# A message-passing layer on one core: pairs of edge blocks share a loaded stretch of the node table, and PE's general path is moved behind the body's code

## The chip, the cores and the metric

One core of a Trainium2 chip runs the whole kernel. Its engines are TensorE (PE in the profile), VectorE (DVE), ScalarE (ACT), GpSimd (POOL) and SyncE (SP), which here only starts transfers. The metric is device time in microseconds of one execution, without the profiler: the median of several runs. The profile is one further execution with the profiler on.

## The reference

6250 nodes with 128 features, 100,000 edges sorted by `dst` (`dst = int(6250 * u**2)` for uniform u, so low nodes have many edges and the last ones about 8 each), `src` at random. In short:

```python
row, col = edge_index                     # src, dst
h = relu(concat(x[row], x[col]) @ Wm1 + bm1)      # hidden 256
h = relu(h @ Wm2 + bm2)
messages = h @ Wm3 + bm3
agg = segment_sum(messages, col) / clip(count, 1.0)[:, None]
upd = relu(concat(x, agg) @ Wn1 + bn1) @ Wn2 + bn2
out = layernorm(x + (x + upd))
```

## The kernel before

**Tables first.** `Wm1` is split by rows, so that the first layer of a message is A[src] + B[dst], with A and B products of x. The prologue makes `a_table` (256 values a node) and `b_table` (two parts, high and low, of 256 values a node, so two table rows a node) in DRAM, in groups `g` of 4 x 128 nodes, one loop of all engines over `g`. In between it reads the edges, turns `dst` into numbers relative to each block's lowest node and into words that later steer the loops.

**Edges in.** Edges are cut into blocks of `EB` = 256, 391 of them (`NBE`), padded to 392 (`NB`). They are loaded into `edges_in` with block `g * BG + p` in partition `p`, column group `g` (`GR` = 4 groups, `BG` = 98 blocks in each). The list `loads` (L444 to 455) cuts `dst` and `src` into transfers of up to 98 rows, and SP issues them at L479, after the first three loads of x. POOL waits for all of them at L607, converts both to floats (L608 source, L612 destination), and DVE takes the lowest and highest node of each block from that (`first_and_last`, L824 and L827, in its step g = 2, ahead of its other work for that group). DVE also makes `rel16`, destination less the block's lowest (`make_relative`, L849), and the words `words_sp`, `words_act`, `words_pe`, `words_dve` (`ranges_and_spans`, L891 to 898, and what follows). SP stores minimum and maximum to `mm_dram` (L518), fetches them back as one row (L522), and stores `rel16` to `rel_dram` (L526).

**The body** takes the blocks in turn, `U` = 4 in one pass of a hardware loop; passes 0, 1 and the last are written out apart (`bodies`). For block k:

- SP loads the pair's relative destinations `rel` (on even k, L543) and the 128 table rows (64 nodes) from the block's lowest node on into `b_win[k % 4]` (L547), when PE has expanded block k - 4 (`s_ex`; an even block waits for k - 3 too, since `rel` is shared by the pair).
- POOL gathers `a_table` rows by `src`, 128 edges in one indirect transfer, two for a block (L630), when block k - 4 has been expanded.
- DVE compares `rel` with the node numbers of the window and gets `onehot_t` (`make_onehot_t`, L1023), two blocks ahead.
- PE transposes the gathered rows into a PSUM bank (L1413) and adds `b_win` x `onehot_t` (`expand`, L1324): the first layer.
- ACT applies relu (`h1`, L732), DVE takes the low part (L1106); PE multiplies by `Wm2` in parts (L1437, 12 matmuls, for block k - 2); ACT and DVE again relu (L740) and low part (L1118); ACT puts the bias in the next bank ahead (L721).
- PE sums edges by node: `onehot` (DVE, L1038) times h2, for block k - 6, four matmuls (L1341, L1345, L1347, L1349) into one of two banks of `sums`, until the block's range of nodes ends. Then PE goes on in the other bank, and DVE adds the old one to `agg` (L1060).

**Far windows.** A block whose nodes span more than the 64 of its window has `far` = (highest - lowest) >> 6 above 0. For each further 64 nodes ACT loads another 128 table rows into `b_far` (`load_far`, in the step before), DVE makes another one-hot at the end of its step, PE waits for both (`expand_far`) and adds two more matmuls.

**PE's word.** One word per block tells PE all exceptions together: far windows of block k, a range that ended before block k - 6, ranges after that. If it is 0 only the straight path is needed:

```python
with pe.If(word > 0):        # L1418
    expand_and_sum(i, k, word)          # the general path
with pe.If(word < 1):        # L1420
    expand(...); first_sum(...); other_sums(...)
```

After the blocks, the end computes the node update and the layernorm in groups g.

Of the kernel before, what the change touches and what calls it, by code (L numbers as in the profile page):

```python
# [34 lines left out]
def gnn_layer(nc, x, src, dst, Wm1, bm1, Wm2, bm2, Wm3, bm3, Wn1, bn1, Wn2, bn2, out):  # L35
# [25 lines left out]
    with ExitStack() as ctx:  # L61
# [20 lines left out]
        words_sp = sb("words_sp", [1, NB], I32)  # L82
# [91 lines left out]
        row_more = carve(NB).bitcast(I32)  # L174
        row_step, row_end = carve(NB).bitcast(I32), carve(NB).bitcast(I32)
# [8 lines left out]
        minmax_i = carve(2 * GR).bitcast(I32)  # L184
        first_quarter = carve(GR).bitcast(I32)
# [47 lines left out]
        s_mm = sem("s_min_max")  # L233
        s_wi = sem("s_min_max_int")
# [27 lines left out]
        s_bw = [sem(f"s_b_win_loaded{c}") for c in range(RB)]  # L262
# [198 lines left out]
        def _(sp):  # L461
# [15 lines left out]
            for n, g, row, rows, edges in loads:  # L477
                at, e0 = (n * GR + g) * EB, (g * BG + row) * EB
# [26 lines left out]
            for g in range(1, NG + 1):  # L505
# [9 lines left out]
                if g == 3:  # L515
                    sp.wait_ge(s_wi, 1)
                    for j in range(GR):
                        sp.dma_start(mm_dram[j * BG:(j + 1) * BG, :], minmax_i[0:BG, 2 * j:2 * j + 2]  # L518
                                     ).then_inc(s_scr, 16)
                if g == 4:  # L520
                    sp.wait_ge(s_scr, 16 * GR)
                    sp.dma_start(row_in[0:1, :], mm_dram.rearrange("(o b) c -> o (b c)", o=1)).then_inc(s_row, 16)  # L522
                if g == 5:
                    sp.wait_ge(s_rel16, 1)
                    for j in range(GR):
                        sp.dma_start(rel_dram[j * BG:(j + 1) * BG, :],  # L526
                                     rel16[0:BG, j * EB:(j + 1) * EB]).then_inc(s_scr_rel, 16)

            sp.wait_ge(s_scr_rel, 16 * GR)
# [7 lines left out]
            def body(i):  # L537
                first = load_words(sp, words_sp, i * U, U, PAD_DST)
                for k in range(U):
                    if there(i, k - RB):  # L540
                        sp.wait_ge(s_ex, i * U + (k - RB + (2 if k % 2 == 0 else 1)))
                    if k % 2 == 0:
# [971 lines left out]
```

## Time and profile before

| | |
|---|---|
| median of 3 runs | 1201.61 us (1199.98 to 1201.78) |
| the profiled execution, its span from first to last instruction | 1416.6 us |
| granted TensorE clock, mean | 0.993 |
| PE busy | 1249.7 us, 88% |
| weight loads of PE busy | 1172.0 us, 83% |
| DVE busy | 979.6 us, 69% |
| ACT busy | 740.6 us, 52% |
| POOL busy | 786.5 us, 56% |
| moved by the DMA engines | 211.4 MB, mean 149 GB/s |

The profiled execution is 215.0 us longer than the median of the runs; it has no other time than its span. Busy is the time in which the engine has at least one instruction of its own at work. The share of the chain is the part of the span that the last chain of dependent work spent on an engine; "issue" in it is time in which the engine waited for nothing that the profile shows. In the timeline, a row is one instruction or a run of like ones, with start, duration, and in brackets the idle time before it.

### The profile page before, as it was taken

Reading aid. Unit: us, or ns where it says so; the run is one execution under the profiler, and the core shown is the slowest. Engines: PE = TensorE matmul, PEld = TensorE weight load, DVE = VectorE, ACT = ScalarE, POOL = GpSimd, SP = SyncE. Lnnn points to the kernel's source line nnn. Section 1 sums busy time; section 2 is a strip of 40 time slices with the busy share of each in tenths; the row PEclk is TensorE's granted clock in tenths of the full one; section 3 lists DMA queues with packets and bytes.
Section 4 is the critical chain, followed back from the end, with each engine's and each line's share of the span. In section 5 each row is a group of like instructions: output and inputs, shape, how many; then the busy total and the mean of one; then the engine's idle time right before and its main releaser. Section 6 shows DMA issues by size and latency. Waiting matters only on the chain.

```text
span 1416.6 us, 33766 instructions
## 1 busy us (share of the span) xinstructions
PE 1249.7 (88%) x9614; PEld 1172.0 (83%) x9615; DVE 979.6 (69%) x2072; ACT 740.6 (52%) x1392; POOL 786.5 (56%) x814
## 2 busy tenths in 40 slices
PE   6978888888888888888888889988999989899997
PEld 6868888888888888888888888888888888888886
DVE  6846666766766666766766766767767767777676
ACT  3544555555555555555555555555554555545585
POOL 2166666666666666666666666666666666564000
PEclk9999999999999999999999999999999999999999
DMA  9665555545545555555545555455545454554022
GB/s 308 274 234 156 146 144 151 149 141 151 151 140 150 152 142 147 151 143 147 152 139 150 146 143 151 145 144 152 139 147 151 138 150 144 145 151 142 10 67 86
DMA packets 135605, 211.42 MB, mean 149 GB/s; under 512 B 24247, under 2 KB 102669, under 8 KB 134030
## 3 DMA queue, kind: packets, MB, share of 16 engines
q1 hardware_dynamic: 98030, 108.43, 25.3%
q0 software_dynamic: 37536, 102.55, 25.1%
q8 instruction: 14, 0.23, 0.1%
q14 instruction: 25, 0.20, 0.0%
HBM read 188.09 MB, written 22.80 MB: 149 GB/s over the span
## 4 chain that ended last, share of the span: by engine, by line
PE 80%; issue 12%; DVE 2%; SPq 1%; another core or an unknown queue 1%; DMA 1%; ACT 1%; DVEq 1%; ACTq 0%
PE bank L1437 39%; PE bank L1413 11%; PE bank L1324 6%; PE sums L1345 4%; PE sums L1341 4%; PE sums L1347 3%; PE sums L1349 3%; PE bank L1478 2%; PE sums L1491 1%; PE bank L1234 1%; PE bank L1219 1%; PE bank L1461 1%; PE sums L1219 1%; DMA b_win<-b_table 1%
## 5 line engine op out<-in xcount | busy, mean ns | idle before, releaser
L630 POOL DMA_INDIRECT a_edge<-a_table,src_idx x782 | 767.1, 981 | 457.8 <-remote 268.2
L1437 PE MATMUL bank<-w,h 128*128 128x256 f32 x4692 | 661.4, 283 | 104.9 <-issue 102.1
L1437 PEld LDWEIGHTS bank<-w,h 128*128 128x128 f32 x4692 | 596.5, 188 | 119.7 <-issue 118.7
L1106 DVE SCALAR_TENSOR_TENSOR h<-bank,h 128x512 fp32r<-128x512 f32 x391 | 268.7, 687 | 338.4 <-issue 326.7
L732 ACT ACTIVATE h<-bank 128x512 fp32r<-128x512 f32 x391 | 233.8, 598 | 475.3 <-remote 439.2
L721 ACT COPY bank<-b_bc 128x512 f32<-128x512 f32 x391 | 231.5, 592 | 115.2 <-issue 66.7
L1118 DVE SCALAR_TENSOR_TENSOR h_lo<-bank,h_hi 128x512 fp32r<-128x512 f32 x391 | 266.5, 681 | 0.1
L1413 PE MATMUL bank<-ident,a_edge 128*128 128x128 f32 x1564 | 237.4, 274 | 21.1 <-issue 16.6
L740 ACT ACTIVATE h_hi<-bank 128x512 fp32r<-128x512 f32 x391 | 232.6, 595 | 2.8 <-PE bank L1437 2.8
L1413 PEld LDWEIGHTS bank<-ident,a_edge 128*128 128x128 f32 x1564 | 180.3, 140 | 40.5 <-issue 34.2
L1324 PE MATMUL bank<-onehot_t,b_win 128*128 128x256 f32 x782 | 190.3, 325 | 0.0
L1038 DVE SCALAR_TENSOR_TENSOR onehot<-iota,first_node,dst_col 128x256 fp32r<-128x256 int16 x391 | 186.0, 476 | 0.4 <-PE sums L1349 0.3
L1023 DVE TENSOR_SCALAR onehot_t<-rel,node_half 128x256 fp32r<-128x256 int16 x391 | 154.7, 396 | 22.0 <-DMA rel<-rel_dram 2.9
L1341 PE MATMUL sums<-h_hi,onehot 128*128 128x258 f32 x391 | 115.8, 296 | 15.0 <-issue 12.3
L1324 PEld LDWEIGHTS bank<-onehot_t,b_win 128*128 128x128 f32 x782 | 118.6, 192 | 3.3 <-issue 1.0
L1345 PE MATMUL sums<-h_lo,onehot 128*128 128x256 f32 x391 | 116.3, 298 | 1.0
L1347 PE MATMUL sums<-h_hi,onehot 128*128 128x258 f32 x391 | 110.4, 282 | 0.0
L1349 PE MATMUL sums<-h_lo,onehot 128*128 128x256 f32 x391 | 109.6, 280 | 0.0
L1341 PEld LDWEIGHTS sums<-h_hi,onehot 128*128 128x128 f32 x391 | 73.4, 188 | 25.1 <-issue 24.8
L1345 PEld LDWEIGHTS sums<-h_lo,onehot 128*128 128x128 f32 x391 | 73.7, 189 | 13.0 <-issue 12.6
L1347 PEld LDWEIGHTS sums<-h_hi,onehot 128*128 128x128 f32 x391 | 74.2, 190 | 0.0
L1349 PEld LDWEIGHTS sums<-h_lo,onehot 128*128 128x128 f32 x391 | 73.4, 188 | 0.0
(190 smaller groups left out, 682.7 us busy)
## 6 DMA issues: line engine op xcount, KB each, us to landing
b_win<-b_table SPq DMA_DIRECT2D x391, 128.0 KB
rel<-rel_dram SPq DMA_DIRECT2D x196, 128.0 KB
a_edge<-a_table,src_idx POOLq DMA_INDIRECT x782
a_table<-work SPq DMA_DIRECT2D x12, 512.0 KB, 4.6
b_table<-work SPq DMA_DIRECT2D x5, 1024.0 KB
b_table<-h SPq DMA_DIRECT2D x4, 1024.0 KB
f_x<-in_x SPq DMA_DIRECT2D x12, 256.0 KB, 5.2
b_table<-a_edge SPq DMA_DIRECT2D x3, 1024.0 KB, 5.8
```

What stands on the lines that cost most here:

```text
L630: pool.indirect_dma_start(a_edge[:, b % R * TB + t, :], None, a_table, bass.IndirectOffsetOnAxis(ap=src_idx[:, b * TB + t:b * TB + t + 1], ...
L721: act.copy(bank[H2[k % U]][:, :], b2_bc[:, :, :].rearrange("p t h -> p (t h)")).then_inc(s_bias, 1)
L732: act.activation(h1[:, k % U, 0, :], bank[k % 2][:, :], ACT.Relu).then_inc(s_h1h, 1)
L740: act.activation(h2_hi[:, (k - LAG) % U, :, 0:H], bank[H2[(k - LAG) % U]][:, :].rearrange("p (t h) -> p t h", t=TB), ACT.Relu).then_inc(s_ ...
L1106: dve.scalar_tensor_tensor(h1[:, k % U, 1, :], bank[k % 2][:, :], 0.0, h1[:, k % U, 0, :].bitcast(F32), ALU.max, ALU.subtract).then_inc(s_ ...
L1118: dve.scalar_tensor_tensor(h2_lo[:, j, :, :], bank[H2[j]][:, :].rearrange("p (t h) -> p t h", t=TB), 0.0, h2_hi[:, j, :, 0:H].bitcast(F32) ...
L1324: ins = pe.matmul(bank[k % 2][:, h * EB:(h + 1) * EB], rows[:, h * P:(h + 1) * P], hot, start=False, stop=True, skip_group_check=True)
L1341: return pe.matmul(to[:, 0:HC], onehot[:, slot, 0, :], h2_hi[:, k % U, 0, :], start=start, stop=False, skip_group_check=True)
L1345: pe.matmul(to[:, 0:H], onehot[:, slot, 0, :], h2_lo[:, k % U, 0, :], start=False, stop=False, skip_group_check=True)
L1347: pe.matmul(to[:, 0:HC], onehot[:, slot, 1, :], h2_hi[:, k % U, 1, :], start=False, stop=False, skip_group_check=True)
L1413: ins = pe.matmul(bank[k % 2][:, h * EB + t * P:h * EB + (t + 1) * P], a_edge[:, k % R * TB + t, h * P:(h + 1) * P], ident[:, :], start=(t ...
L1437: ins = pe.matmul(to, h1[:, j, a, h * EB + t * P:h * EB + (t + 1) * P], w2[:, b, h, :], start=False, stop=(a == 1 and h == KH - 1), skip_g ...
```

## The change

Four things are done. The 128-row stretch of `b_table` is loaded once for two blocks, from the lower of their lowest nodes, and `rel16`, `words_sp` and `far` are taken relative to that. The edges lie in `edges_in` with two neighbouring blocks side by side in one partition, and so are loaded in rows of 512 edges; the stores to `mm_dram` and `rel_dram` become two each. ACT's copies of the transposed edges are rearranged to match. And on PE the general path is emitted after the straight code of the whole pass, reached by a branch, with a branch back.

```diff
-        full = E // EB
-        assert (GR - 1) * BG <= full
+        full = E // (2 * EB)
+        assert (GR // 2 - 1) * BG <= full < GR // 2 * BG
         loads = []
         for n in range(2):
-            for g in range(GR):
-                rows = min(full - g * BG, BG)
+            for a in range(GR // 2):
+                rows = min(full - a * BG, BG)
                 if rows:
-                    loads.append((n, g, 0, rows, EB))
-            if E % EB:
-                loads.append((n, GR - 1, rows, 1, E % EB))
+                    loads.append((n, a, 0, rows, 2 * EB))
+            if E % (2 * EB):
+                loads.append((n, GR // 2 - 1, rows, 1, E % (2 * EB)))
...
-            for n, g, row, rows, edges in loads:
-                at, e0 = (n * GR + g) * EB, (g * BG + row) * EB
+            for n, a, row, rows, edges in loads:
+                at, e0 = (n * GR + 2 * a) * EB, (a * BG + row) * 2 * EB
...
-                    for j in range(GR):
-                        sp.dma_start(mm_dram[j * BG:(j + 1) * BG, :], minmax_i[0:BG, 2 * j:2 * j + 2]
-                                     ).then_inc(s_scr, 16)
+                    for a in range(GR // 2):
+                        sp.dma_start(mm_dram[a * 2 * BG:(a + 1) * 2 * BG, :].rearrange("(p c) m -> p (c m)", c=2),
+                                     minmax_i[0:BG, 4 * a:4 * a + 4]).then_inc(s_scr, 16)
...
-                first = load_words(sp, words_sp, i * U, U, PAD_DST)
-                for k in range(U):
-                    if there(i, k - RB):
-                        sp.wait_ge(s_ex, i * U + (k - RB + (2 if k % 2 == 0 else 1)))
...
+                first = load_words(sp, words_sp, i * (U // 2), U // 2, PAD_DST)
+                for c in range(RC):
+                    if there(i, 2 * c - U):
+                        sp.wait_ge(s_ex, i * U + (2 * c - U + 2))
+                    sp.dma_start(rel[:, c, :].rearrange("p (b e) -> p b e", b=2),
+                                 rel_dram[bass.ds(i * U + 2 * c, 2), :].partition_broadcast(P)
+                                 ).then_inc(s_rc[c], 16)
+                    sp.dma_start(b_win[:, c, :].bitcast(F32),
+                                 b_table[bass.ds(first[c] * 2, P), :]).then_inc(s_bw[c], 16)
...
-            pool.memset(edges_in[:, (GR - 1) * EB:GR * EB], PAD_DST).then_inc(s_pad, 1)
-            pool.memset(edges_in[:, (2 * GR - 1) * EB:2 * GR * EB], 0).then_inc(s_pad, 1)
+            pool.memset(edges_in[:, (GR - 2) * EB:GR * EB], PAD_DST).then_inc(s_pad, 1)
+            pool.memset(edges_in[:, (2 * GR - 2) * EB:2 * GR * EB], 0).then_inc(s_pad, 1)
...
+                dve.tensor_tensor(pair_low[0:BG, :], minmax[0:BG, 0:2 * GR:4], minmax[0:BG, 2:2 * GR:4], ALU.min
+                                  ).then_inc(s_mm, 1)
...
-                dve.tensor_copy(words_sp[0:1, :], lowest).then_inc(s_rw, 1)
-                dve.tensor_tensor(far, highest, lowest, ALU.subtract).then_inc(s_rw, 1)
+                dve.tensor_tensor(words_sp[0:1, :], row_in[0:1, 0:2 * NB:4], row_in[0:1, 2:2 * NB:4], ALU.min
+                                  ).then_inc(s_rw, 1)
+                dve.tensor_tensor(row_low[0:1, :].rearrange("o (b c) -> o b c", c=2),
...
+                dve.wait_ge(s_low, 1)
+                dve.tensor_tensor(far, highest, row_low[0:1, :], ALU.subtract).then_inc(s_rw, 1)
...
                 if k % 2 == 0:
                     dve.wait_ge(s_rc[k // 2 % RC], nth(i, k, 16))
-                dve.wait_ge(s_bw[k % RB], nth(i, k, 16))
+                    dve.wait_ge(s_bw[k // 2 % RC], nth(i, k, 16))
...
-                        with pe.If(word > 0):
-                            expand_and_sum(i, k, word)
-                        with pe.If(word < 1):
-                            expand(b_win[:, k % RB, :], onehot_t[:, k % 2, :], k).then_inc(s_ex, 1)
...
+                        outer[k] = nc.cur_bb
+                        pe.br_cmp(word, 0, on_true=label(i, k, "apart"), on_false=label(i, k, "straight"),
+                                  comp_op="IS_GT")
+                        nc.switch_bb(label(i, k, "straight"), parent=outer[k])
+                        expand(b_win[:, k // 2 % RC, :], onehot_t[:, k % 2, :], k).then_inc(s_ex, 1)
+                        to = bank_at(own)
+                        first_sum(to, (k - BACK) % U, k - BACK, False)
+                        ins = other_sums(to, (k - BACK) % U, k - BACK)
+                        if among_last(i, k - BACK, BACK + 1):
+                            ins.then_inc(s_sg, 1)
+                        pe.br(label(i, k, "joined"))
+                        nc.switch_bb(label(i, k, "joined"), parent=outer[k])
...
+                last = nc.cur_bb
+                pe.br(label(i, 0, "ended"))
+                for k in steps(i, BACK + 1):
+                    if there(i, k) and there(i, k - BACK - 1):
+                        with nc.body(label(i, k, "apart"), parent=outer[k], valid_engines=bass.OrderedEngineSet([pe.engine])):
+                            expand_and_sum(i, k, words[k])
+                            pe.br(label(i, k, "joined"))
+                nc.switch_bb(label(i, 0, "ended"), parent=last)
```

The stores to `rel_dram` change as those to `mm_dram` do.

## Rows read from the trace of the kernel before

**Rows 1.** The page, parts 1 and 4: busy time, and the chain that ended last.

```profile
PE 1249.7 (88%) x9614; PEld 1172.0 (83%) x9615; DVE 979.6 (69%) x2072; ACT 740.6 (52%) x1392; POOL 786.5 (56%) x814
...
PE 80%; issue 12%; DVE 2%; SPq 1%; another core or an unknown queue 1%; DMA 1%; ACT 1%; DVEq 1%; ACTq 0%
```

**Rows 2.** Windows: stretch, its length, busy time (count), granted clock, DMA share, GB/s.

```profile
core 0: us, PE busy (x) PEld busy (x) DVE busy (x) ACT busy (x) POOL busy (x), PEclk, DMA share, GB/s
0.00:89.40 89.40, 69.46 (x446) 62.58 (x447) 63.73 (x115) 41.92 (x79) 24.89 (x37) 0.96 0.81 293
89.40:1308.00 1218.60, 1081.74 (x8533) 1023.51 (x8534) 840.62 (x1673) 632.09 (x1164) 760.61 (x776) 1.00 0.51 147
...
600.75:602.35 1.60, 0.37 (x1) 0.19 (x1) 0.52 (x1) 0.00 (x0) 0.74 (x1) 1.00 0.72 230
```

**Rows 3.** Timeline of PE in the body: start, duration, line, operation.

```profile
628.18 0.48 PE L1324 MATMUL bank<-onehot_t,b_win 128*128 128x256 f32 x2
...
628.98 1.58 PE L1437 MATMUL bank<-w,h 128*128 128x256 f32 x12
...
631.54 0.28 PE L1437 MATMUL bank<-w,h 128*128 128x256 f32 x1
```

**Rows 4.** The groups view (part 5 of the page): count, busy, mean ns, idle before.

```profile
L630 POOL DMA_INDIRECT a_edge<-a_table,src_idx x782 | 767.1, 981 | 457.8 <-remote 268.2
...
L1324 PE MATMUL bank<-onehot_t,b_win 128*128 128x256 f32 x782 | 190.3, 325 | 0.0
...
L1023 DVE TENSOR_SCALAR onehot_t<-rel,node_half 128x256 fp32r<-128x256 int16 x391 | 154.7, 396 | 22.0 <-DMA rel<-rel_dram 2.9 <-DMA b_win<-b_table 1.6 <-issue 0.7
```

**Rows 5.** Timeline of the engines over two blocks of the body.

```profile
605.33 0.95 POOL L630 DMA_INDIRECT a_edge<-a_table,src_idx  x1 [0.30 <-issue]
605.43 0.59 ACT L721 COPY bank<-b_bc 128x512 f32<-128x512 f32 x1 [0.75 <-issue]
...
605.55 0.48 PE L1324 MATMUL bank<-onehot_t,b_win 128*128 128x256 f32 x2
...
606.72 0.68 DVE L1118 SCALAR_TENSOR_TENSOR h_lo<-bank,h_hi 128x512 fp32r<-128x512 f32 x1
```

**Rows 6.** The DMA view: count, KB each, median us from issue to landing.

```profile
f_x<-in_x SPq DMA_DIRECT2D x12, 256.0 KB, 5.2
...
a_table<-work SPq DMA_DIRECT2D x1, 128.0 KB, 3.5
...
f_x<-in_x SPq DMA_DIRECT2D x1, 53.0 KB
```

**Rows 7.** The lines of PE's two branches: durations ns, least, median, most.

```profile
L1418 PEldq COMPARE_BRANCH  x384: 68/204/338, 108.2 to 1307.6; - x192
...
L1420 PEldq COMPARE_BRANCH  x384: 72/73/202, 108.6 to 1307.9; - x192
```

**Rows 8.** The DMA view from 130 to 1300 us: queues, packets, MB, share.

```profile
q1 hardware_dynamic: 80681, 73.48, 22.1%
q14 instruction: 5, 0.04, 0.0%
```

**Rows 9.** Windows of the prologue, columns as in rows 2.

```profile
10.00:15.00 5.00, 5.00 (x40) 5.00 (x40) 3.13 (x5) 2.25 (x4) 2.03 (x2) 1.00 1.07 342
...
15.00:30.00 15.00, 9.73 (x69) 9.07 (x67) 12.58 (x22) 6.42 (x15) 0.00 (x0) 0.89 1.03 391
```

**Rows 10.** Timeline of the prologue, POOL and DVE.

```profile
11.48 1.04 POOL L608 CAST agg<-a_edge 98x1024 f32<-98x1024 int32 x1 [5.07 <-DMA a_edge<-in_src]
...
13.54 0.70 DVE L824 TENSOR_SCALAR agg<-a_edge 98x1024 int32<-98x1024 int32 x1 [0.33 <-POOL agg L612]
...
23.28 1.29 DVE L979 TENSOR_TENSOR work<-bank,rel 128x512 f32<-128x512 f32 x2 [2.18 <-DMA a_table<-work]
```

**Rows 11.** Timeline of the prologue, DVE's work on one row.

```profile
39.65 0.55 DVE L893 TENSOR_TENSOR agg<-agg 1x392 int32<-1x392 int32 x1
```

**Rows 12.** Timeline of SP's queue in the prologue: issues.

```profile
26.26 5.35 SPq L518 DMA_DIRECT2D mm_dram<-agg  x4
...
38.82 3.12 SPq L526 DMA_DIRECT2D rel_dram<-agg  x4
```

More of the change, by code:

```diff
@@ L184, in gnn_layer @@
         minmax_i = carve(2 * GR).bitcast(I32)
+        pair_low = carve(GR // 2)
         first_quarter = carve(GR).bitcast(I32)
@@ L233, in gnn_layer @@
         s_mm = sem("s_min_max")
+        s_low = sem("s_lowest_of_pairs")
         s_wi = sem("s_min_max_int")
@@ L261, in gnn_layer @@
         s_rc = [sem(f"s_rel_loaded{c}") for c in range(RC)]
-        s_bw = [sem(f"s_b_win_loaded{c}") for c in range(RB)]
+        s_bw = [sem(f"s_b_win_loaded{c}") for c in range(RC)]
         s_bf = sem("s_b_far_loaded")
@@ L524, in _ @@
                     sp.wait_ge(s_rel16, 1)
[L525 to L529, printed above, removed]
+                    for a in range(GR // 2):
+                        sp.dma_start(rel_dram[a * 2 * BG:(a + 1) * 2 * BG, :].rearrange("(p c) e -> p (c e)", c=2),
+                                     rel16[0:BG, a * 2 * EB:(a + 1) * 2 * EB]).then_inc(s_scr_rel, 16)
+            sp.wait_ge(s_scr_rel, 16 * (GR // 2))
             sp.wait_ge(s_bz, 16)
@@ L537, in body @@
             def body(i):
-                first = load_words(sp, words_sp, i * U, U, PAD_DST)
-                for k in range(U):
-                    if there(i, k - RB):
-                        sp.wait_ge(s_ex, i * U + (k - RB + (2 if k % 2 == 0 else 1)))
-                    if k % 2 == 0:
-                        sp.dma_start(rel[:, k // 2, :].rearrange("p (b e) -> p b e", b=2),
-                                     rel_dram[bass.ds(i * U + k, 2), :].partition_broadcast(P)
-                                     ).then_inc(s_rc[k // 2], 16)
-                    if there(i, k):
-                        sp.dma_start(b_win[:, k % RB, :].bitcast(F32),
-                                     b_table[bass.ds(first[k] * 2, P), :]).then_inc(s_bw[k % RB], 16)
+                first = load_words(sp, words_sp, i * (U // 2), U // 2, PAD_DST)
[7 more added lines that the diff above has]
+                                 b_table[bass.ds(first[c] * 2, P), :]).then_inc(s_bw[c], 16)
             bodies(sp, body)
@@ L645, in edge_columns @@
                     act.wait_ge(s_et, n * GR + g // 2 * 2 + 2)
-                    act.copy(col[:, g * BG * TB:(g + 1) * BG * TB].rearrange("p (b t) -> p t b", t=TB),
+                    act.copy(col[:, g // 2 * 2 * BG * TB:(g // 2 + 1) * 2 * BG * TB]
+                             .rearrange("p (b c t) -> p c t b", c=2, t=TB)[:, g % 2, :, :],
                              bank[6 + g // 2][:, g % 2 * TB * BG:(g % 2 + 1) * TB * BG]
@@ L847, in make_relative @@
             def make_relative():
-                dve.tensor_tensor(rel16[0:BG, :].rearrange("p (g e) -> p g e", g=GR), dst_f,
-                                  minmax[0:BG, 0:2 * GR:2].unsqueeze(2).to_broadcast([BG, GR, EB]), ALU.subtract
+                dve.wait_ge(s_mm, 3)
+                dve.tensor_tensor(rel16[0:BG, :].rearrange("p (a e) -> p a e", a=GR // 2),
+                                  dst_f.rearrange("p (a c) e -> p a (c e)", c=2),
+                                  pair_low[0:BG, :].unsqueeze(2).to_broadcast([BG, GR // 2, 2 * EB]), ALU.subtract
                                   ).then_inc(s_rel16, 1)
@@ L902, in first_words @@
                 dve.wait_ge(s_rw, 6)
-                dve.scalar_tensor_tensor(words_act[0:1, 0:NB], far, float(2**13), lowest, ALU.mult, ALU.add
+                dve.scalar_tensor_tensor(words_act[0:1, 0:NB], far, float(2**13), row_low[0:1, :], ALU.mult, ALU.add
                                          ).then_inc(s_rw, 1)
@@ L1402, in expand_and_sum, with label @@
                     sum_all_further(k - BACK - 1, word)
+            def label(i, k, what):
+                return f"pe_body{i if isinstance(i, int) else 'loop'}_block{k}_{what}"
             def body(i):
                 words = load_words(pe, words_pe, i * U, words_of(i, BACK + 1), PE_TOP)
+                outer = {}
                 for k in steps(i, BACK + 1):
```

16 lines of the change are left out of this document (8 added, 8 removed).

## The prediction

> **What bounds the kernel now.** I read the page first: TensorE (PE) is busy 88% of the span and holds 80% of the chain that ended last, with 12% put down to "issue" [rows 1]. So I asked what PE does in a block and what the "issue" is. The windows give three stages: a prologue of 89.4 us that builds the tables, a body of 391 blocks until 1308.0, and an end of 108.6 us [rows 2]. PE's timeline in the body shows a block without a hole: L1437 begins at 628.98 and again at 631.54, 2.56 us, matmuls back to back between [rows 3]; I call such blocks free, and take 2.57. But the body's mean is 1218.6/391 = 3.12 us. The difference, some 214 us, sits in pauses in which all engines stop at once: between 600.75 and 602.35 PE begins one matmul, VectorE (DVE) ends one operation and ScalarE (ACT) does nothing [rows 2]. PE then resumes within a batch of L1437, which waits for no semaphore, so no dependency of the kernel explains it. The runs' median, 1201.61 us, is 215.0 us below the profiled span of 1416.6, and 89.4 + 391 x 2.57 + 108.6 = 1202.9: the runs outside the profiler are what the trace gives without its pauses. So PE bounds the body at 2.57 us a block, and the body has next to nothing to win unless a matmul goes. None does. The terms below are microseconds of a stage; I add them to the profiled span and to the median alike, without scaling.
>
> GpSimd (POOL) is close behind PE: two gathers a block of 981 ns, and 0.30 between [rows 4, 5], 2.56 us. DVE has 840.6/391 = 2.15 us a block [rows 2].
>
> **The change part by part.**
>
> *Half the loads of the node table.* 195 loads of 128 KB go. DVE waited 1.6 us in all for a loaded window [rows 4], the DMA engines are 51% busy in the body [rows 2]: the loads lie under PE's matmuls. Were the body bound by the gathers instead, fewer loads would not shorten POOL's 981 ns. Bounds 0 and -2 us; I take 0.
>
> *A pair's second block reaches beyond 64 nodes.* The window starts at the lower of two lowest nodes. From the reference's inputs I worked out `(highest - lowest of the pair) >> 6`: it is 1 for blocks 383, 387 and 389, and 0 for the rest; before it was 0 for all, as L1324's 782 = 2 x 391 matmuls say [rows 4]. Each of the three now takes the far path: ACT loads 128 KB, DVE makes one more one-hot after its step, PE waits for both and runs two more matmuls. In a free stretch PE wants the next expansion at 605.55, while DVE is done with its step at 606.72 + 0.68 = 607.40 and needs 0.40 for the one-hot [rows 4, 5]: 2.25 us late. ACT's COPY begins at 605.43 [rows 5]; behind it ACT reads its word and issues, and a 128 KB transfer landed in 3.5 us at the quickest [rows 6]: some 4 us late. PE is the bound, so its wait stays. Bounds for one: 0.24 us (all covered, two matmuls of 0.12) and 4.5 us; I take 3, so 3 x 3 = +9 us, bounds +1 and +14.
>
> *PE's general path behind the body's code.* In the records of PE's sequencer L1418 takes 204 ns, jumping over the general path, and L1420 73 ns [rows 7]. The new straight block keeps one untaken compare and at most one plain branch: 0.2 us less, 316 times. In free blocks that lies under matmuls issued before it: from L1324 on there is no hole [rows 3]. The blocks that end a range (62 before, 65 now, worked out from the inputs) take a jump of 204 ns there and one back, +0.2 us each, under the same matmuls. Sum 0. Bounds: all straight jumps exposed -63 us, for which the 1202.9 against 1201.6 leaves no room; all general ones exposed +13 us.
>
> A rule speaks against this edit. Between 130 and 1300 us the queue that brought PE's code in 16 KB pieces carries nothing, and the other code queue 0.04 MB [rows 8], though PE jumps back over the whole body every fourth block. By these rows a jump to the end of the body costs 0.2 us and no transfer. The Trainium skill (Runtime: NRT & Kernel Launch, Instruction fetch mechanics) says that a taken branch to code outside a window of two pages waits for a DMA. That is rival 4, priced there from rows.
>
> *Edge loads in pairs of blocks.* Here is what I expect to decide. Before, `dst` and `src` each come in loads of 98, 98, 98, 96 and 1 rows of 256 edges. After, 100000/512 = 195 rows of 512 edges are cut into 98, 97 and 1. What matters is over how many DMA engines a load is spread. The trace's semaphore events say it: a 128-row load of x raises its semaphore 16 times as data lands; the load of x's last 106 rows raises it once at issue and twice on landing, at 20.00 and 20.17; the ten edge loads raise theirs 126 times, which is 6 x (14 + 1) + 2 x 16 + 2 x (1 + 1). So 128 rows use 16 engines, 98 use 14, 96 use 16, 106 use 2 and 1 uses 1: the largest divisor up to 16. (The DMA view gives a landing for the 256 KB loads and none for the 53 KB one [rows 6], since it looks for 16 steps.) 97 is prime: one engine carries 97 x 2 KB = 199 KB, twice.
>
> An engine's rate: all 16 at full share move 342 to 391 GB/s [rows 9], 21.4 to 24.4 each. 199 KB take 8.1 to 9.3 us, two in a row 16.3 to 18.6. Before, 800 KB over all engines took 50 KB each, 2.0 to 2.3 us. So the edges are complete 14 to 16.5 us later than now, less up to 1.5 for four SP issues that go. If the two run on different engines it is 6 to 7 us. No row decides which; nothing in the trace shows engines taking turns, so I take the same engine, +14 us.
>
> Who waits: POOL's L608 waits for all edge loads; it waited 5.07 us already and began at 11.48. DVE's L824 stands behind it at 13.54 with 0.33 us to spare [rows 10], and DVE goes in order: the rest of group 2 (the low part of x, the copies of both products) is queued behind it, and PE behind that. Later transfers queue on the same engine, above all the store of a_table whose landing ended DVE's wait of 2.18 us at 23.28 [rows 10]; it moves along. DVE is busy 12.58 of 15 us from 15 on [rows 9], so little can be caught up. I keep all 14.
>
> The Trainium skill (DMA: Bandwidth & Descriptors, Why a DMA increments its semaphore by 16 and not by 1) states the same divisor rule and that HWDGE takes the lowest-numbered engines. The trace's counts agree with the first; the second no row shows. By the page the sum would be the same.
>
> *The rest of the prologue.* DVE gets a minimum of 98x4, one over 196 in place of a copy over 392, and one over 392 like L893, 0.55 us [rows 11], with its wait: +1 us in all, DVE being on the path (bounds 0 and +1.5). Two stores fewer to `mm_dram` and two to `rel_dram`, where SP spent 5.35 and 3.12 us on four each [rows 12], under PE's and DVE's work: -1 to 0, I take -0.6. POOL's two larger memsets end before SP comes to wait for them: 0.
>
> Sum: 1201.6 + 14 + 9 + 1 + 0 - 0.6 = 1225.0. A little may be caught up; I say **1224 us**.
>
> **The rivals.**
> 1. *The two prime loads run side by side*: +6 in place of +14, so 1217. For it: no row names the engine. Chance 0.12.
> 2. *The edges are no problem*: the 97 rows are cut otherwise. Then +9 and +1: 1211, or 1203 with the far blocks at their low bound. Against it: the 106-row load. 0.08.
> 3. *Faster*: PE's sequencer, not the matmuls, bounds the body outside the profiler. What decides is the share of the 316 straight jumps that is exposed: all give -63 us, and from 26 us on (0.4 of them) it outweighs the rest; with 40 us, 1184. Against it: [rows 3] and the sum of 1202.9. 0.11.
> 4. *General blocks pay for the far jump*: 65 x 0.2 = +13, 1237; with a code transfer each of 3.5 us, like the quickest of [rows 6], +228, 1452. Against it: [rows 8]. 0.06.
>
> The forecast has 0.63.
>
> **How the numbers follow.** A measurement of this kernel tells about 0.2%, 2.4 us. The likeliest case by its bounds: 1201.6 + 12 + 1 - 1 = 1214 to 1201.6 + 16.5 + 14 + 1.5 = 1234. To hold eight in ten I go down over rival 1 and most of 2 to 1206 and up to 1237. Faster 0.12 (rival 3 and a little of 2), same 0.05 (the low end of 2 and a partial 3), slower 0.83.
>
> **What would show it.** After the change L608 starts near 25 us, its wait ended by a load of `src`, and the body's first transposes near 104, not 89.4. Free blocks stay at 2.57 us. L1324's successor has 788 matmuls, with holes of 2 to 4 us before the far ones. There are 196 window loads. The prediction is wrong if L608's successor starts before 16 us, if free blocks fall under 2.5, or if the body grows by more than 14 us.

## The result, and the profile after

The kernel after takes **1241.47 us** (median of 4 runs, 1240.39 to 1243.82) against 1201.69 (1199.98 to 1201.94) on the same chip: a ratio of 1.0332, 95% interval 1.0318 to 1.0347. It is slower, as predicted, but by 39.8 us instead of 22, outside the range (1206 to 1237).

The page of the kernel after, its busy times and its chain (they answer to [rows 1]):

```profile
PE 1183.9 (95%) x9620; PEld 1158.4 (93%) x9621; DVE 962.5 (78%) x2077; ACT 742.0 (60%) x1392; POOL 771.6 (62%) x814
...
PE 90%; DMA 4%; DVE 2%; issue 2%; POOL 1%; SPq 1%; ACT 0%; DVEq 0%; ACTq 0%
```

This profile has no pauses: its span of 1240.3 us is the run's own time less 1.9. So the difference can't be read against the profile of before with its 215 us of pauses. I took a new profile of the kernel before (first experiment); its span is 1200.1. Windows of the kernel after, cut at the first transposes of blocks 0, 20, 380 and 390 (columns as in [rows 2]):

```profile
0.00:104.47 104.47, 71.81 (x446) 64.32 (x448) 64.36 (x117) 43.13 (x79) 24.86 (x36) 0.87 0.68 250
...
104.47:157.44 52.97, 49.86 (x393) 48.82 (x393) 36.79 (x74) 30.88 (x56) 39.28 (x42) 0.94 0.54 153
157.44:1088.34 930.90, 930.69 (x7923) 927.56 (x7922) 763.63 (x1556) 586.04 (x1080) 692.37 (x721) 1.00 0.53 152
1088.34:1133.19 44.85, 33.65 (x228) 31.94 (x227) 25.35 (x53) 16.36 (x31) 14.11 (x15) 0.85 0.38 103
...
1133.19:1240.30 107.11, 97.89 (x638) 85.75 (x636) 72.32 (x279) 65.58 (x147) 0.99 (x2) 0.98 0.17 54
```

and of the new profile of the kernel before, cut at the same blocks:

```profile
0.00:88.72 88.72, 69.09 (x447) 62.23 (x448) 63.71 (x115) 41.97 (x79) 24.59 (x37) 0.96 0.81 295
...
88.72:140.49 51.77, 49.30 (x393) 48.35 (x394) 36.40 (x74) 30.78 (x56) 39.39 (x41) 0.93 0.62 183
140.49:1066.65 926.16, 926.16 (x7922) 926.15 (x7921) 767.67 (x1556) 594.85 (x1080) 700.67 (x721) 1.00 0.61 178
1066.65:1092.47 25.82, 25.82 (x222) 25.78 (x221) 22.21 (x46) 16.46 (x30) 14.44 (x15) 1.00 0.62 181
...
1092.47:1200.10 107.63, 98.47 (x638) 85.90 (x636) 74.22 (x283) 66.26 (x149) 0.99 (x2) 0.98 0.17 54
```

Read the first number after each stretch, its length. The prologue is 15.8 us longer, blocks 0 to 19 are 1.2, blocks 20 to 379 are 4.7, **the ten blocks from 380 are 19.0 us longer**, the end is 0.5 shorter: 40.2 us. The last ten also show PE at a granted clock of 0.85. The prologue is what was predicted; the body was to grow by 9 us and grows by 25.

*The prologue.* POOL's first cast of the edges, two rows of SP's queue (the three issues for `src`, and the next load of x), and DVE's step that waits for a store of a_table (they answer to [rows 10]):

```profile
25.49 1.04 POOL L609 CAST agg<-a_edge 98x1024 f32<-98x1024 int32 x1 [18.66 <-DMA a_edge<-in_src]
...
5.24 10.31 SPq L482 DMA_DIRECT2D a_edge<-in_src  x3
15.59 0.36 SPq L467 DMA_DIRECT2D f_x<-in_x  x1
...
37.05 1.29 DVE L991 TENSOR_TENSOR work<-bank,rel 128x512 f32<-128x512 f32 x2 [1.87 <-DMA a_table<-work]
```

The cast begins 14 us later than in [rows 10]. In the trace's semaphore events, the edges' semaphore takes 38 steps, 2 x (14 + 1) + 4 x (1 + 1): each 97-row load uses one engine. Its steps pause between 16.35 and 25.23 us, 8.9 us, before the last two: the second of these loads lands that much behind the first.

*The first block of the last pass.* PE's timeline, and behind it the view of the branch's line in PE's sequencer, for this block (durations in ns, least, median, most; first and last start):

```profile
1115.46 0.60 PE L1430 MATMUL bank<-ident,a_edge 128*128 128x128 f32 x4
1121.19 0.80 PE L1336 MATMUL bank<-onehot_t,b_win 128*128 128x256 f32 x2 [5.13 <-issue]
...
1123.29 2.76 PE L1458 MATMUL bank<-w,h 128*128 128x256 f32 x12
```

```profile
L1436 PEldq COMPARE_BRANCH  x1: 5444/5444/5444, 1115.3 to 1115.3; - x1
```

That is block 388, and it ends a range: PE stands 5.13 us at "issue", because its sequencer's jump to the general path took 5.4 us. L1458's twelve matmuls then take 2.76 us instead of 1.58: the granted clock was at the lower level after the hole (0.50 from 1121.2 to 1126 us). It is not a far block. The queue that brings PE's code in 16 KB packets, silent from 136 to 1117 us, shows in the DMA view from 1100 to 1135:

```profile
q8 instruction: 5, 0.08, 1.1%
```

The first of the five packets begins at 1118.4 us, within the jump. Block 389's branch takes 5.2 us too, from 1123.0 on, with packets that begin at 1124.2 and 1124.7.

*A block of the loop that ends a range and begins a pass* (block 56), in the kernel after and in the new profile of before, PE's first three sums:

```profile
250.72 0.34 PE L1353 MATMUL sums<-h_hi,onehot 128*128 128x258 f32 x1
251.07 0.38 PE L1357 MATMUL sums<-h_lo,onehot 128*128 128x256 f32 x1
251.29 0.28 PE L1359 MATMUL sums<-h_hi,onehot 128*128 128x258 f32 x1
```

```profile
233.77 0.29 PE L1341 MATMUL sums<-h_hi,onehot 128*128 128x258 f32 x1
233.89 0.28 PE L1345 MATMUL sums<-h_lo,onehot 128*128 128x256 f32 x1
234.01 0.28 PE L1347 MATMUL sums<-h_hi,onehot 128*128 128x258 f32 x1
```

From the start of the first to the start of the third it is 0.57 us after and 0.24 before, and the block takes 2.90 us. There are 16 such blocks in the loop, all of them 2.84 to 2.92 us, and they are the 4.7 us of the middle. Blocks that end a range elsewhere in a pass cost nothing more.

*The far blocks.* PE, DVE and ACT at block 383, and PE's groups (they answer to [rows 4]):

```profile
1098.81 0.66 PE L1336 MATMUL bank<-onehot_t,b_far 128*128 128x256 f32 x2 [2.16 <-DVE onehot_t L1042]
...
1097.39 0.49 DVE L1072 SCALAR_TENSOR_TENSOR agg<-sums,from_quarter,agg  x1
1098.33 0.35 DVE L1042 TENSOR_SCALAR onehot_t<-rel,node_half 128x256 fp32r<-128x256 int16 x1 [0.45 <-issue]
...
1095.63 0.40 ACTq L719 DMA_DIRECT2D b_far<-b_table  x1
```

```profile
L1336 PE MATMUL bank<-onehot_t,b_win 128*128 128x256 f32 x782 | 189.8, 324 | 5.1 <-issue 5.1
L1336 PE MATMUL bank<-onehot_t,b_far 128*128 128x256 f32 x6 | 1.7, 363 | 5.9 <-DVE onehot_t L1042 3.7 <-issue 2.2
```

788 matmuls and three holes, as predicted. Blocks 383, 387 and 389 are 4.2, 2.3 and 4.8 us longer than 2.57, but 389's hole is put down to "issue": its branch of 5.2 us ended last, most of it under the slow matmuls of block 388. With the path back in the body (inline, below) DVE's one-hot ends 389's hole, which is as long (2.12 us), and the block is still 4.3 us longer: most of it is the far window's.

### The profile page after: what moved, and what is told of

The parts are those of the page before. It is cut to its first block, busy times and chain, and to the rows that moved or that the text cites. A ratio compares the mean times of both kernels' runs of the same rounds, so it can differ in the third digit from the quotient of the medians.

```text
span 1240.3 us, 32750 instructions
## 1 busy us (share of the span) xinstructions
PE 1183.9 (95%) x9620; PEld 1158.4 (93%) x9621; DVE 962.5 (78%) x2077; ACT 742.0 (60%) x1392; POOL 771.6 (62%) x814
## 4 chain that ended last, share of the span: by engine, by line
PE 90%; DMA 4%; DVE 2%; issue 2%; POOL 1%; SPq 1%; ACT 0%; DVEq 0%; ACTq 0%
PE bank L1458 44%; PE bank L1430 13%; PE bank L1336 8%; PE sums L1357 4%; PE sums L1353 4%; PE sums L1359 4%; PE sums L1361 4%; PE bank L1508 3%; PE sums L1521 2%; DMA a_edge<-in_src 1%; PE bank L1246 1%; DMA a_table<-work 1%; PE bank L1491 1%; POOL a_edge L631 1%; PE bank L1231 1%
## 5 line engine op out<-in xcount | busy, mean ns | idle before, releaser
L631 POOL DMA_INDIRECT a_edge<-a_table,src_idx x782 | 751.8, 961 | 266.4 <-issue 151.4
L1458 PE MATMUL bank<-w,h 128*128 128x256 f32 x4692 | 622.8, 282 | 0.0
L1458 PEld LDWEIGHTS bank<-w,h 128*128 128x128 f32 x4692 | 586.7, 190 | 0.0
L1035 DVE TENSOR_SCALAR onehot_t<-rel,node_half 128x256 fp32r<-128x256 int16 x391 | 141.9, 363 | 38.4 <-DMA b_win<-b_table 19.6
L1353 PE MATMUL sums<-h_hi,onehot 128*128 128x258 f32 x391 | 112.1, 287 | 0.4 <-issue 0.2
L1357 PE MATMUL sums<-h_lo,onehot 128*128 128x256 f32 x391 | 112.0, 286 | 0.2
L1359 PE MATMUL sums<-h_hi,onehot 128*128 128x258 f32 x391 | 111.3, 285 | 0.0
L1361 PE MATMUL sums<-h_lo,onehot 128*128 128x256 f32 x391 | 110.2, 282 | 0.0
```

Source lines behind the costliest of these rows:

```text
L631: pool.indirect_dma_start(a_edge[:, b % R * TB + t, :], None, a_table, bass.IndirectOffsetOnAxis(ap=src_idx[:, b * TB + t:b * TB + t + 1], ...
L1353: return pe.matmul(to[:, 0:HC], onehot[:, slot, 0, :], h2_hi[:, k % U, 0, :], start=start, stop=False, skip_group_check=True)
L1357: pe.matmul(to[:, 0:H], onehot[:, slot, 0, :], h2_lo[:, k % U, 0, :], start=False, stop=False, skip_group_check=True)
L1359: pe.matmul(to[:, 0:HC], onehot[:, slot, 1, :], h2_hi[:, k % U, 1, :], start=False, stop=False, skip_group_check=True)
L1361: return pe.matmul(to[:, 0:H], onehot[:, slot, 1, :], h2_lo[:, k % U, 1, :], start=False, stop=True, skip_group_check=True)
L1458: ins = pe.matmul(to, h1[:, j, a, h * EB + t * P:h * EB + (t + 1) * P], w2[:, b, h, :], start=False, stop=(a == 1 and h == KH - 1), skip_g ...
```

## The experiments

"Start" is where the first transposes of block 0 lie; "loop" and "last ten" are what blocks 20 to 379 and 380 to 389 take beyond 2.57 us each, from the starts of PE's transposes in each kernel's profile. The kernels ran in several batches, each beside runs of the kernel before; so a price in the text is a difference of ratios, times 1201.7 us, and is uncertain by some 2 us. "Start" varies too, each from one profile: after and six kernels with the same prologue have it at 102.8 to 105.4 us.

| kernel | median us | ratio to before, interval | start | loop | last ten |
|---|---|---|---|---|---|
| before, again | 1201.99 (1 run) | | 88.7 | 1.0 | 0.1 |
| after | 1241.47 | 1.0332 (1.0318-1.0347) | 104.5 | 5.7 | 19.2 |
| split96 | 1226.46 | 1.0203 (1.0189-1.0217) | 92.9 | 5.8 | 18.2 |
| split_src_only | 1234.49 | 1.0257 (1.0241-1.0273) | 98.1 | 5.6 | 19.5 |
| before_cut97 | 1209.18 | 1.0051 (1.0036-1.0067) | 96.8 | 0.9 | 0.1 |
| inline | 1228.36 | 1.0221 (1.0208-1.0235) | 105.4 | 1.1 | 11.1 |
| before_moved | 1213.43 | 1.0106 (1.0089-1.0123) | 89.2 | 5.8 | 7.3 |
| near_code | 1229.92 | 1.0218 (1.0204-1.0233) | 104.9 | 2.3 | 9.7 |
| loop_only | 1232.66 | 1.0252 (1.0236-1.0268) | 104.6 | 5.7 | 9.0 |
| split_inline | 1214.85 | 1.0106 (1.0091-1.0120) | 90.4 | 1.2 | 10.0 |
| far_first | 1211.40 | 1.0076 (1.0063-1.0090) | 90.7 | 0.9 | 7.8 |
| all_three | 1204.70 | 1.0017 (1.0008-1.0026) | 90.4 | 0.9 | 0.1 |
| gap_256 | 1242.09 | 1.0326 (1.0296-1.0356) | 105.1 | 5.7 | 18.6 |
| gap_1024 | 1251.31 | 1.0403 (1.0342-1.0464) | 102.8 | 13.9 | 18.3 |

**The kernel before, again.** Nothing is edited.

> The kernel before, unchanged, for a profile without the pauses in which all engines stop. Theory A (the split into 89.45 us of prologue, 390 blocks of 2.57 us and 108.6 us of end holds): first transposes near 89.5 us, first block of a pass at 2.57 us whether general or not, general blocks in the last pass within 0.5 us of the others. Theory B (the prologue was stretched by a pause, so that the change costs more than 15 us there): first transposes near 84 to 87 us. In the last pass the kernel before should show no hole of PE above 2 us under theory C (the hole of 5.1 us at block 388 is the jump's) and one of the same size under its rival (the hole belongs to the last pass whatever the code's place).

Theory A holds: 88.7 us, and theory C: no hole, 2.67 us for block 388. Code packets come in this last pass too (one begins at 1091.0 us), but PE doesn't wait for them.

**split96.** Both 97-row loads are cut.

```diff
-                if rows:
-                    loads.append((n, a, 0, rows, 2 * EB))
+                if rows % 2 == 0:
+                    loads.append((n, a, 0, rows, 2 * EB))
+                else:
+                    loads.append((n, a, 0, rows - 1, 2 * EB))
+                    loads.append((n, a, rows - 1, 1, 2 * EB))
```

> After, with each edge load of 97 rows cut into one of 96 rows and one of 1 row. Theory (the 97-row load of 2 KB rows goes through one DMA engine, 16 us for the two of them in series): the start comes back by 14 us, the first transposes lie near 90 us, the kernel takes 1241.5 - 14 = 1227.5 us (1225 to 1230). Rival (the loads of 2 KB rows themselves, or what stands behind them in SP's order, are slow): under 4 us come back, 1238 us or more.

15.5 us come back, as the theory had it. **split_src_only** cuts the load of `src` alone (`if rows % 2 == 0 or n == 0`):

> After, with the 97-row load of src alone cut into 96 and 1 rows; dst's stays whole. Theory (each whole 97-row load occupies one DMA engine for about 8 us, the two in series): half of the 15 us comes back, 1241.5 - 7.5 = 1234 us (1232 to 1236). Rival (one slow load is enough, since both would run side by side on different engines): nothing comes back, 1241 us; or the src load alone was the slow one: 1226.5 us.

About half comes back: 9.0 us by the runs, 6.4 by the start. **before_cut97** puts the number into the kernel before: the second load of each tensor, 98 rows of 1 KB, becomes one of 97 and one of 1.

```diff
-                if rows:
+                if g == 1:
+                    loads.append((n, g, 0, rows - 1, EB))
+                    loads.append((n, g, rows - 1, 1, EB))
+                elif rows:
                     loads.append((n, g, 0, rows, EB))
```

> The kernel before, with the second 98-row load of dst and of src each cut into 97 rows and 1 row (rows of 1 KB, two DMAs more). Theory (a DMA of 97 rows goes through one engine; 97 packets of 42 to 84 ns each are 4.1 to 8.1 us, two in series 8 to 16 us): the first transposes come 4 to 13 us later than 88.7 us, the kernel takes 1206 to 1215 us, most likely 1209 us. Rival (rows of 2 KB or the paired layout make the loads slow, not the count of 97): 1202 to 1203.5 us, the two added DMAs costing at most 1 us.

It costs 6.1 us, and the start moves by 8.1. POOL's first cast in four profiles, before again, split96, split_src_only, before_cut97:

```profile
10.87 1.04 POOL L608 CAST agg<-a_edge 98x1024 f32<-98x1024 int32 x1 [4.47 <-DMA a_edge<-in_src]
```

```profile
12.74 1.04 POOL L612 CAST agg<-a_edge 98x1024 f32<-98x1024 int32 x1 [5.91 <-DMA a_edge<-in_src]
```

```profile
18.93 1.04 POOL L612 CAST agg<-a_edge 98x1024 f32<-98x1024 int32 x1 [11.57 <-DMA a_edge<-in_src]
```

```profile
18.56 1.04 POOL L611 CAST agg<-a_edge 98x1024 f32<-98x1024 int32 x1 [12.14 <-DMA a_edge<-in_src]
```

The cast begins at 10.9, 12.7, 18.9 and 18.6 us, and in the kernel after at 25.5. Each whole 97-row load of 2 KB rows adds 6 to 7 us; in before_cut97, two of them with half the bytes each add 7.7. So the count of 97 rows is the cause, in rows of either size and in either layout, and the loads run in series.

**inline.** The general path goes back into the pass, as before; all else is as after.

```diff
-                        outer[k] = nc.cur_bb
-                        pe.br_cmp(word, 0, on_true=label(i, k, "apart"), on_false=label(i, k, "straight"),
-                                  comp_op="IS_GT")
-                        nc.switch_bb(label(i, k, "straight"), parent=outer[k])
...
+                        with pe.If(word > 0):
+                            expand_and_sum(i, k, word)
+                        with pe.If(word < 1):
```

> After, with PE's general path back inside the body, as in the kernel before; shared window and edge loads as after. Theory (the jump behind the body costs a fetch of code in passes that are executed for the first time, 5.4 us of branch and 2.5 us of low clock at block 388, and 0.3 us at each of 16 general blocks that begin a pass): 1241.5 - 8 - 5 = 1228.5 us. Theory with the fetch alone, the 0.3 us belonging to the beginning of a pass in any code: 1233.5 us. Rival (block 388's hole comes with a cold last pass in either layout): 1241.5 us, within 2 us.

13.3 us come back, the number of the first theory, and block 388 takes 2.58 us (its transposes begin at 1110.76, the next ones at 1113.34). **before_moved** is the opposite: the kernel before with this part of the diff alone.

> The kernel before, with PE's general path moved behind the body's code and nothing else. Theory (fetch at cold code plus 0.3 us at general blocks that begin a pass): 1201.7 + 8 to 13 = 1210 to 1215 us. Rival (the place of the code is free, and the losses of the kernel after come from the shared window): 1201.7 us, within 2 us.

It costs 12.7 us; the profile has 4.8 of it in the loop and 7.2 in the last ten, where block 388 again has the hole (4.21 us). The rival is out: the place of the code costs this without a shared window too.

**near_code.** Each general path stands right behind its own block's code, still reached by a jump.

```diff
                         pe.br(label(i, k, "joined"))
+                        with nc.body(label(i, k, "apart"), parent=outer[k], valid_engines=bass.OrderedEngineSet([pe.engine])):
+                            expand_and_sum(i, k, words[k])
+                            pe.br(label(i, k, "joined"))
...
-                pe.br(label(i, 0, "ended"))
```

> After, with each general path standing directly behind its own block's code, still reached by a taken jump and left by another; the jump at the end of each pass is gone. Theory A (what costs is that the jump goes far, to code not yet at hand): block 388 comes back to 2.6 us, and of the 0.3 us at general blocks that begin a pass at least the part of the jump at the pass's end (0.17 us) goes: 1241.5 - 7.8 - (3 to 5) = 1229 to 1231 us. Rival B (any taken jump into the general path costs, near or far): block 388 stays at 10.4 us, 1239 to 1241.5 us. With A right for the last pass and the 0.3 us due to the taken branch alone: 1233.5 us.

13.7 us come back, block 388 takes 3.11 us, and so a jump as such is cheap. The loop's part shows in the sequencer's instructions that open a range (the line's view gives their start), at block 56, set against the first transposes of the block (timeline). The kernel after, near_code, and before again:

```profile
L1385 PEldq FUSED_REGOPS  x1: 180/180/180, 250.4 to 250.4; - x1
```

```profile
250.04 0.60 PE L1430 MATMUL bank<-ident,a_edge 128*128 128x128 f32 x4
```

```profile
L1385 PEldq FUSED_REGOPS  x1: 183/183/183, 249.4 to 249.4; - x1
```

```profile
249.24 0.60 PE L1430 MATMUL bank<-ident,a_edge 128*128 128x128 f32 x4
```

```profile
L1373 PEldq FUSED_REGOPS  x1: 183/183/183, 233.1 to 233.1; - x1
```

```profile
233.09 0.60 PE L1413 MATMUL bank<-ident,a_edge 128*128 128x128 f32 x4
```

Against the block's transposes the sequencer is 0.4 us late, 0.2 us late and level. All 16 blocks agree: 0.34 to 0.40 us late, 0.13 to 0.18 late, and level within 0.04. At range-ending blocks elsewhere in a pass the sequencer is ahead, mostly by 0.5 us in before again and by 0.2 to 0.4 in after. At the head of a pass the sequencer has just done the loop's branch and the load of the words, and has no lead left; what the jump at a pass's end and the taken compare add there, shows. **loop_only** keeps the path behind the body in the loop and puts it back into the passes that are written out.

```diff
-                    if there(i, k) and there(i, k - BACK - 1):
+                    if there(i, k) and there(i, k - BACK - 1) and isinstance(i, int):
+                        with pe.If(word > 0):
+                            expand_and_sum(i, k, word)
...
+                    elif there(i, k) and there(i, k - BACK - 1):
                         outer[k] = nc.cur_bb
```

> After, with the general path back in the body in the three passes that are written out (the first two and the last), behind the body in the loop alone. Theory (two prices: 7.8 us for the jump in the last pass, 4.8 us at the 16 general blocks that begin a pass of the loop, where PE's sequencer loses its lead): 1241.5 - 7.8 = 1233.7 us, the loop's 16 blocks still at 2.85 to 2.92 us. Rival (the jump at block 388 is dear because its path is reached for the first time after a long loop, wherever that path stands): 1241 us.

9.6 us come back; the loop keeps its 5.7. The rival is out: block 388 reaches its general path for the first time here too, inside the body, and takes 3.49 us. So the move has two prices: about 5 us in the loop, 7 to 10 us in the last pass.

**split_inline** joins split96 and inline; **all_three** also keeps far windows from arising (`far` shifted by 7 bits instead of 6).

> After, with the 97-row loads cut into 96 and 1 rows and PE's general path back in the body; the far windows stay. If the parts add: 1241.5 - 15.0 - 13.1 = 1213.4 us, and its distance to the kernel without far windows is their whole price, 11.3 us by the blocks of after's trace (8.5 to 12).

> After, with the 97-row loads cut into 96 and 1 rows, PE's general path back in the body, and no far windows (the contributions of the 64 nodes beyond the shared window are left out in blocks 383, 387 and 389). If the four causes add and the halved window loads are worth nothing: 1241.5 - 15.0 - 13.1 - 11.3 = 1202.1 us, within 2 us of before. If the halved loads gave something that the other parts hid: under 1199 us. If another cost of the shared window is left (a first transpose at 92.9 us after split96 against 88.7 us speaks for up to 4 us): 1204 to 1206 us.

The two differ by 0.89% of the time, 10.7 us, and by 9.9 us in the last ten: that is the price of the three far windows. all_three is still 0.17% (0.08 to 0.26) over before, the third of the cases expected: some 2 us remain unexplained, and the halved loads bring nothing that shows. Its loop and last ten are those of the kernel before and its start is 1.7 us later, so the rest lies in the prologue if that is more than the spread of one profile; no run settles it.

**far_first.** In split_inline, DVE makes the far one-hot before its other work of the block.

```diff
                             make_onehot_t(i, k + 2)
+                        if there(i, k + 1):
+                            with dve.If((word & (127 * 2**9)) > 0):
+                                far_onehots_t(k + 1, word)
```

> The kernel with 96 and 1 rows and the path in the body, with DVE's far one-hot made right behind the one-hot of the second next block and not behind the range's additions. Theory (PE's hole of some 2 us ahead of a far block is DVE's order: its far one-hot comes last): the hole falls to under 0.5 us, and with it part of the low clock: 11.3 us fall to 3 to 6 us, 1206 to 1208 us. Rival (the hole is the far window's load from HBM, 2.1 to 2.7 us): no change, 1213.4 us.

Both were wrong. 3.6 us come back, 2.3 of them in the profile's last ten. The holes ahead of the three far blocks shrink little, from 1.85, 1.39 and 1.88 us to 1.71, 1.43 and 1.34, since the load of the far window is as late as DVE was; another 1.2 us is that the twelve matmuls of block 383 were at the lower clock in split_inline's profile (2.76 us) and are not here (1.58). That the load was nearly last already stands in the kernel after, in the weight load of block 383; behind it PE at block 383 in far_first:

```profile
1098.81 0.37 PEld L1336 LDWEIGHTS bank<-onehot_t,b_far 128*128 128x128 f32 x2 [2.39 <-DMA b_far<-b_table]
```

```profile
1079.26 0.51 PE L1339 MATMUL bank<-onehot_t,b_far 128*128 128x256 f32 x2 [1.71 <-DMA b_far<-b_table]
```

**padded, gap_256, gap_1024.** Why does the jump of block 388 wait, when 63 jumps of the loop don't? Counted in the program, it goes over 417 instructions, the loop's over some 180. padded was to put never executed code between:

> After, with 1,024 instructions that are never executed between the loop's body and the general paths behind it, so that each of the loop's 62 jumps goes further. Theory (a jump is dear when it leaves the code that is at hand, and the loop's body with its general paths is all at hand; distance decides): each general block of the loop now pays a fetch of 2 to 5 us out and, where nothing hides it, another back: 1241.5 + 60 x (2 to 10) = 1360 to 1800 us, with code packets all through the body. Rival (distance is nothing, only code executed for the first time is fetched; the paths of the loop are fetched once): 1241.5 to 1260 us.

It took 1240.79 us (one run), but the stretch was not in the program that ran (its code queue brought 17 packets, as in after; in gap_1024 it brought 21), so it tells nothing. The other two put it under a branch that is never true:

```diff
                             expand_and_sum(i, k, words[k])
+                            if k == 0 and not isinstance(i, int):
+                                with pe.If((words[k] & 127) > 100):
+                                    for _ in range(2560):
+                                        pe.reg_add(more, more, ended)
```

(2,560 additions become 256 instructions; 10,240 become 1,024.)

> After, with a branch behind the general path of a pass's first block in the loop, and 256 instructions under it that are never executed. Counted in the program, the jump from the body to the other three general paths then goes over some 440 instructions where it went over some 180; in the last pass of the kernel after the jump of block 388 goes over 417. 47 blocks of the loop take such a jump, and the 16 first ones come back over the gap. Theory (distance decides: such a jump leaves the code at hand and fetches for some 5 us, with 2 to 3 us of low clock behind it): 1241.5 + 47 x 5 to 8 = 1480 to 1620 us, with code packets in the body. Rival (only the first execution of a path is dear, wherever it stands): 1241.5 to 1260 us.

> The same with 1,024 instructions under the branch, so that the jumps go over some 1,200 instructions and the loop with its general paths is four times as long. Theory of distance: as with 256 or dearer, 1480 to 1700 us. Rival (first execution): 1241.5 to 1260 us. Should 256 cost nothing and 1,024 hundreds of us, then what is at hand is a store larger than 440 instructions, and block 388 paid for code that had never been fetched, not for distance.

gap_256 changes nothing that shows. gap_1024, in the range of its rival, pays 8.2 us in the loop, **once**, at block 125, the first block that takes the jump over the gap as second of its pass. Its jump takes 3.8 us. PE there; the view of the branch's line from 434 us on; and the DMA view's queue of code packets, from 424 to 434 us and from 434 to 1100. The packets begin at 426.6, 430.3 and 434.4, the second at the start of the hole of 2.86 us inside the path:

```profile
427.36 0.60 PE L1432 MATMUL bank<-ident,a_edge 128*128 128x128 f32 x4
430.00 0.51 PE L1338 MATMUL bank<-onehot_t,b_win 128*128 128x256 f32 x2 [2.05 <-issue]
433.37 0.58 PE L1355 MATMUL sums<-h_hi,onehot 128*128 128x258 f32 x1 [2.86 <-issue]
```

```profile
L1438 PEldq COMPARE_BRANCH  x259: 64/67/209, 434.2 to 1108.5; - x130
```

```profile
q8 instruction: 2, 0.03, 1.5%
...
q8 instruction: 1, 0.02, 0.0%
```

The other 21 jumps over the same gap from that place in the pass wait at most 0.21 us. Blocks 91 and 115 had jumped over it before, to the path of a pass's fourth block, without a wait; that path lies beside the pass's end, to which the first pass of the loop had jumped in 3.3 us (at 131.2). So distance is not the price: it is code that PE reaches for the first time and that nothing has brought in yet. Block 388 lies in a pass that is executed once, so its jump is always such a one.

## Why the prediction was wrong, step by step

- **PE's general path behind the body's code: "Sum 0".** This step failed. inline and before_moved price it at 13.3 and 12.7 us, near the upper bound of +13, but not by the mechanism that this bound was for (0.2 us at each of 65 blocks), so that the two numbers agree is luck. The runs show 0.3 us at each of 16 blocks, 4.8 us in all, and a wait for code in the last pass, 7 to 10 us with the low clock after it. I argued "under the same matmuls" from [rows 3], which shows a free block. At the head of a pass the kernel before had no lead left, as its new profile shows (the wait starts level with the transposes).
- **"A jump to the end of the body costs 0.2 us and no transfer"** [rows 8] was right for the loop and read too widely: a silent code queue over a loop says nothing of a pass that is written out and executed once. The Trainium skill's rule (Runtime: NRT & Kernel Launch, Instruction fetch mechanics), that a taken branch outside a window of two pages of 256 instructions waits for a fetch, foresaw a wait of this kind; but gap_1024's repeated jumps over 1,200 instructions wait for nothing, so here it holds for code reached for the first time, not for every jump of that length. Rival 4 had the right place; neither of its sums (+13 by 65 plain jumps, +228 by a transfer at each) was the mechanism.
- **Edge loads, +14.** Right, in its mechanism too: 15.5 us measured, the cast at 25.49 for "near 25", the first transposes at 104.47 for "near 104". split_src_only settles what no row could, that the two loads run in series, so rival 1 is out, and rival 2 with it; that it is the same engine is argued from this. The Trainium skill (DMA: Bandwidth & Descriptors, Why a DMA increments its semaphore by 16 and not by 1) has such a load on the lowest-numbered engine; two one-engine loads in series agree with that.
- **Far blocks, +9.** Right blocks, right size: 9.9 to 10.7 us measured. My reading of the cause was incomplete, and the size is partly luck: the holes are shorter than forecast (1.5 to 2.2 us for "2 to 4"), and much of the rest is the low clock behind some of them (2.38 us for 1.58 at block 383), which the prediction didn't have.
- **Half the loads, 0.** Right: all_three is not faster than before.
- **The rest of the prologue, +0.4.** What all_three leaves, some 2 us, is the most that it can be; its cause stays open.
- **Rival 3**, a sequencer that bounds the body, is out: free blocks still take 2.57 us.

Of its own signs of being wrong, one came true: the body grew by 25 us, more than 14.

With 13 us for the code's place the sum would have been 1201.6 + 14 + 9 + 0.4 + 13 = 1238 against 1241.5; the remaining 3 us are no more than the small overruns of the other three terms.

No version here beats the kernel before; of those with the shared window that do all of the reference's work, far_first comes nearest, 0.76% slower.

## What to carry to other kernels

Before moving a rare path out of line, look at the instruction stream where the sequencer has least lead (the head of a loop pass, just after the loop's branch and its loads of words), and at passes that are executed once; a free block in the middle tells nothing of either. Cut DMAs so that the row count has a large divisor up to 16: cutting each of two 97-row loads into 96 and 1 gave back 15.5 us. Loads that were hidden already are not worth halving when the price is paid on the engine that bounds the kernel.

## What the runs showed of the hardware

- Loads on one DMA engine also hold up SP's queue: the three issues for `src` took 10.31 us where five take 1.91 in before again and four take 1.45 in split96, and the next load of x went out at 15.59 us instead of 7.17 and 6.14. The last of the three is a single row and took 7.5 us.
- A jump of PE to code not yet fetched took 3.3 to 6.8 us (3.3 to the end of the loop's pass in gap_1024, 6.8 at block 388 of split_src_only); later jumps over gap_1024's gap took 0.21 us at most.
- Holes of PE of some 2 us have the lower clock level behind them in some profiles and not in others. At block 383, twelve matmuls take 2.38 us behind a hole of 2.16 (after) and 2.76 behind 1.85 (split_inline), but 1.58, the upper level's time, behind 2.26 (gap_256). So a far block is 2 to 3 us longer or about 4, and nothing read here tells beforehand which. Behind the holes of 3.7 to 6.5 us at block 388 the twelve always took longer, 2.38 to 2.76.
